# Part of the learnt activation between attention passes moves to GpSimd, and VectorE's other part comes one chunk later

## The reference

```python
h = _transformer_conv(x, src, dst, edge_attr, Wq0, bq0, ...)   # attention: out / (s + 1e-16) + x @ Ws + bs
h = jnp.where(h >= 0, h, prelu_a * h)
h = _transformer_conv(h, src, dst, edge_attr, Wq1, bq1, ...)
h = jnp.where(h >= 0, h, prelu_a * h)
h = _transformer_conv(h, src, dst, edge_attr, Wq2, bq2, ...)
```

## Time and profile before

| | us |
|---|---|
| median of three runs (lowest, highest) | 6334.99 (6330.81, 6335.18) |
| the profiled execution | 6323.52 |
| its span | 6321.9 |
| TensorE busy in it | 5535.2 (88%) |
| VectorE busy | 5521.8 (87%) |
| GpSimd busy | 4377.9 (69%) |
| ScalarE busy | 2824.9 (45%) |

### The profile page before, as it was taken

One profiled execution on the slowest core, in us unless ns is written; L12 is line 12 of the kernel. 1 busy time (PEld: TensorE's weight loads), 2 busy tenths in 40 slices (PEclk: granted clock), 3 DMA queues, 4 the chain that ended last, 5 costly groups with the idle time before them and its releaser, 6 DMA issues. The chain is left out here.

```text
span 6321.9 us, 195360 instructions
## 1 busy us (share of the span) xinstructions
PE 5535.2 (88%) x49413; PEld 4085.5 (65%) x49413; DVE 5521.8 (87%) x18582; ACT 2824.9 (45%) x12163; POOL 4377.9 (69%) x4735
## 2 busy tenths in 40 slices
PE   7997888898988887898888889888898888898887
PEld 5775666666666666666666666666666666666665
DVE  6557999989999998998989998988899898989898
ACT  3223555555555555455555555555333333333332
POOL 1223777777777775777777777775777777777775
PEclk9998999999999998999999999999899999999998
DMA  4554433333444343433333333343433343434343
GB/s 127 159 159 112 104 101 100 101 101 101 101 102 103 101 101 101 102 103 101 102 101 101 103 101 101 101 101 96 107 103 102 101 102 101 103 101 101 101 103 80
DMA packets 732932, 662.41 MB, mean 105 GB/s; under 512 B 421004, under 2 KB 558158, under 8 KB 732878
## 3 DMA queue, kind: packets, MB, share of 16 engines
q0 software_dynamic: 148544, 293.76, 19.3%
q1 hardware_dynamic: 555242, 315.06, 18.8%
q10 hardware_dynamic: 29092, 52.97, 2.8%
HBM read 639.39 MB, written 21.78 MB: 105 GB/s over the span
## 5 line engine op out<-in xcount | busy, mean ns | idle before, releaser
L1918 POOL DMA_INDIRECT Gall<-KV,sdn x4440 | 4227.0, 952 | 1376.7 <-issue 1261.8
L1215 ACT ACTIVATE vals<-vj,vals 128x32 f32<-128x32 f32 (+1 forms) x7960 | 1796.8, 313 | 19.3
L1153 PE MATMUL pG<-KVH,ohB 128*128 128x512 f32 (+1 forms) x2586 | 1185.3, 462 | 207.0 <-DVE cont L886 171.3
L1208 ACT ACTIVATE vals<-dd 128x16 f32<-128x16 f32 (+1 forms) x606 | 131.8, 218 | 2686.7 <-DVE dd L1021 2669.6
L1153 PE MATMUL pG<-KVH,ohA 128*128 128x512 f32 (+1 forms) x2613 | 1137.5, 435 | 11.5 <-DVE fm L974 0.6
L1153 PE MATMUL pG<-KVL,ohB 128*128 128x512 f32 (+1 forms) x2586 | 1080.6, 418 | 0.0
L1153 PE MATMUL pG<-KVL,ohA 128*128 128x512 f32 (+1 forms) x2613 | 1019.8, 393 | 0.0
L1146 PE MATMUL pY<-O,vals 128*66 128x42 f32 (+1 forms) x10576 | 783.3, 237 | 0.0
L1153 PEld LDWEIGHTS pG<-KVH,ohB 128*128 128x128 f32 x2586 | 534.2, 207 | 367.3 <-issue 245.0
L1146 PEld LDWEIGHTS pY<-O,vals 128*66 128x66 f32 (+1 forms) x10576 | 710.3, 144 | 46.6 <-ACT vals L1222 34.1
L1153 PEld LDWEIGHTS pG<-KVH,ohA 128*128 128x128 f32 x2613 | 504.6, 193 | 150.8 <-issue 10.9
(11 more groups left out here) (266 smaller groups left out, 8473.0 us busy)
## 6 DMA issues: line engine op xcount, KB each, us to landing
db<-D SPq DMA_DIRECT2D x606, 256.0 KB, 3.5
ea<-in_ea SPq DMA_DIRECT2D x606, 128.0 KB
Gall<-KV,sdn POOLq DMA_INDIRECT x4440
db<-D ACTq DMA_DIRECT2D x202, 256.0 KB, 3.6
qw<-QT SPq DMA_DIRECT2D x1818, 5.2 KB
dr<-in_dr SPq DMA_DIRECT2D x1212, 4.0 KB
ea<-in_ea SPq DMA_DIRECT2D x202, 64.0 KB, 3.6
sdn<-in_sdn SPq DMA_DIRECT2D x606, 12.0 KB
```

The source lines that it names most:

```text
L1153: p = e.matmul(pG[:, 0:128 * m], table[:, n, :], half[:, 4 * q:4 * q + m, :].rearrange("p t c -> p (t c)"), start=n == 0 and h == 0, stop= ...
L1208: return e.activation(vals[u][:, :, 64:64 + H], dd[:, :, 0:H], ACT.Exp, scale=scale)
L1215: i = e.activation(vals[u][:, j, C * h:C * h + C], vj[u][:, j, C * h:C * h + C], ACT.Identity, scale=vals[u][:, j, 64 + h:65 + h])
L1918: e.indirect_dma_start(G[u][:, j, :], None, kvtab, bass.IndirectOffsetOnAxis(ap=sdn[u][:, j:j + 1], axis=0)).then_inc(s_g[u], 16)
```

## The change

`neg` goes from VectorE to GpSimd, behind the two memsets of its chunk, and waits there for VectorE's `val`. `act` leaves `fold_V_ops` and becomes `act_V`, which VectorE runs for chunk n - 1 after the fold of chunk n; it waits for GpSimd's `neg` of chunk n - 1. TensorE's columns of a chunk wait for `act`, as before. GpSimd's memset `one` waits for the `neg` of the chunk before instead of its `clr`, and in the kinds other than `mid` nothing changes.

```diff
-        fold_V = ["den", "rcp", "avg", "val"] + {"mid": ["neg", "act"]}.get(kind, ["xr"])
-        end_V = fold_V[-1]
+        fold_V = ["den", "rcp", "avg", "val"] + {"mid": []}.get(kind, ["xr"])
+        end_V = "act" if kind == "mid" else fold_V[-1]
...
-                oG += [(o, c) for c in fo for o in (("one", "clr") if kind == "mid" else ("clr",))]
+                oG += [(o, c) for c in fo for o in (("one", "clr", "neg") if kind == "mid" else ("clr",))]
                 for c in fo:
                     oP += [("ftr", c)]
                     oV += [(o, c) for o in fold_V]
+            if kind == "mid":
+                oV += [("act", c) for c in co]
...
                 if kind == "mid":
                     if c:
-                        e.wait_ge(own["G"], pG_["clr", c - 1])
+                        e.wait_ge(own["G"], pG_["neg", c - 1])
                     e.memset(hT[64:128, 512 * c:512 * c + 128 * tiles_of[c]], 1.0).then_inc(own["G"], 1)
                     e.wait_ge(own["G"], pG_["one", c])
                 e.memset(acc[:, 512 * c:512 * c + 128 * tiles_of[c]], 0.0).then_inc(own["G"], 1)
+                if kind == "mid":
+                    e.wait_ge(own["V"], pV["val", c])
+                    e.tensor_scalar(SQ[:, cells(c), :], WK[:, cells(c), :], 0.0, pra[:, 0:1],
+                                    ALU.min, ALU.mult).then_inc(own["G"], 1)
...
                 if folds:
                     for c in fo:
                         fold_V_ops(e, c)
+                if kind == "mid":
+                    for c in co:
+                        act_V(e, c)
...
-            else:
-                e.tensor_scalar(skip, val, 0.0, pra[:, 0:1], ALU.min, ALU.mult).then_inc(own["V"], 1)
-                e.wait_ge(own["V"], pV["neg", c])
-                e.scalar_tensor_tensor(val, val, 0.0, skip, ALU.max, ALU.add).then_inc(own["V"], 1)
+
+        def act_V(e, c):
+            e.wait_ge(own["G"], pG_["neg", c])
+            e.scalar_tensor_tensor(WK[:, cells(c), :], WK[:, cells(c), :], 0.0, SQ[:, cells(c), :],
+                                   ALU.max, ALU.add).then_inc(own["V"], 1)
```

More of the change, by code:

```diff
@@ L713, in fold_V_ops @@
             e.tensor_tensor(val, val, skip, ALU.add).then_inc(own["V"], 1)
-            e.wait_ge(own["V"], pV["val", c])
+            if kind != "mid":
+                e.wait_ge(own["V"], pV["val", c])
             if kind == "mean":
```

## The result

The changed kernel takes 6427.65 us, the median of 4 runs (6424.55 to 6435.08), against 6334.51 us (6330.81 to 6335.18, 4 runs) for the kernel before: a ratio of 1.0148, 95% interval 1.0137 to 1.016. It is slower, as predicted, but by 93 us and not by 50, and outside the predicted range.

What follows compares the result with a forecast made beforehand. It took VectorE to pace the node phases, with most time in untouched edge passes. Per phase 1.1 + 23.1 + 2.2 less 1.4 gave 25 us, two phases 50: from 6334.99 to 6385 us, range 6356 to 6402.

Steps and rivals of the forecast that it cites:

- the edge passes unchanged: Attention passes over the edges: the profile after would show them as before, since the change does not touch them.
- The circle: Node phases: VectorE and TensorE no longer overlap, so a chunk takes 4.53 us at half clock, 3.33 at full.
- The sum of a phase: Each node phase: 1.1 + 23.1 + 2.2 = 26.4 us more, less 1.4 for full-clock spells: 25.
- Start: Beginning of a node phase: `act` of chunk 1 comes at 2476.3 instead of 2475.17, +1.1 us.
- Middle: From `act` of chunk 1 to chunk 11: 22.2 us becomes 45.3 at half clock, +23.1, or +11.1 at full.
- End: From `act` of chunk 11 to the first query product: 3.6 us before, +2.2 at half clock, nothing at full.
- spells at full clock: Node phases: short spells of TensorE at full clock give back 1 to 2 us a phase; 1.4 taken off.
- The clock: TensorE in the node phases: half clock (1.2 GHz) for most of both, at 61% busy; chance 67%.
- Full clock as a rival: TensorE at full clock from chunk 4 or sooner: 6359 us, or about 6365 rising where it rose before; chance 17%.
- GpSimd did not become the bound: Rival in the node phases: a slow `neg` of, say, 5 us makes GpSimd the bound, 38 us more, 6423; chance 4%.
- The engines in each other's way: Rival: `neg` starts ahead of `act` and holds it up, about 0.5 us 22 times, 11 us more, 6396; chance 8%.
- VectorE as the bound, not slower: Rival in the node phases: next fold independent of `act`, chunk 1.70 us, 6325 or 6328 in all; chance 4%.

Runs made afterwards that it cites:

- the last run: Kernel before plus 26 GpSimd `tensor_scalar`s in the node phases, writing a spare tile nobody reads: 6370.21 us against 6327.14, ratio 1.007.
- Undone on TensorE's side: Changed kernel with TensorE's transposes of the next sums put ahead of the columns that wait for `act`: 9805.84 us, ratio 1.0005 to the kernel before.
- made alone: Changed kernel with `neg` kept on VectorE in the fold, only `act` one chunk later: 9865.81 against 9804.37 us, ratio 1.0068; again on another chip, 1.006.

## Why the prediction missed

**The step that failed** is its first sentence on what bounds the kernel: "nearly all of it the four passes over the edges, which the change does not touch", and with it "the edge passes unchanged" at its end. The code of the passes is untouched, but their pace is GpSimd's, one gather every 1.25 us, and the gathers became slower, by 14 ns in the median and 11 in the mean. 1480 gathers a pass and three passes make a small thing large: 50.3 of the 100.6 us between the profiled executions, where the prediction had nothing. The prediction never asked what sets the pace of the passes. If it had, it would have read that an increase of 1% in one duration there weighs as much as its whole sum; that the duration would move it could not have read anywhere in the trace of before. The busy shares hide it: GpSimd was busy 69% of the span and TensorE 88%, but 1262 of the 1377 idle us before the gathers are "issue", time in which GpSimd waited for nobody.

What the runs show of it, and how firmly:
- That the passes follow the gathers where GpSimd has nothing to wait for: shown by the last run (33.3 us of passes for 34.8 more of gathers, with the old order in the phases and the clock at 0.94), though from one profile each. It is not the other way round, since on the chips with 3000 us passes the gathers were slower by the same 8 to 14 ns and the passes no longer.
- Which programs have slower gathers: of the 20 profiles, the 8 of the five programs with 26 `tensor_scalar`s on GpSimd in the node phases have medians of 955 to 958 ns, the other 12 of 944 to 947. One such instruction in a phase, 26 at the end, or 26 memsets in the phases don't do it. How many it takes between 1 and 26 was not tried.
- Why, stays open. The gathers are slower from the first, at 587 us, before any `neg` has run in that execution, so it is a matter of the program as a whole, or of what an execution leaves to the next. No run told these two apart.

**The circle was right**, in kind and in size: 4.59 us measured against 4.53. Undone on TensorE's side, it gives back 22 of 25.5 us a phase; made alone, it costs 31. Alone it costs more than in the changed kernel in the main because `neg` is then still in the fold: 4.97 us a chunk, 0.38 more.

**The sum of a phase was right**, in part by luck: 25.5 us measured, 25 predicted. Start: `act` of chunk 1 came 2489.17 - 2482.70 = 6.5 us after the phase began, against 2475.17 - 2470.00 = 5.2 before: +1.3, predicted 1.1. Middle, from there to the `act` of chunk 11 at 2534.52: 45.35 us, predicted 45.3; nine circles were 0.06 longer than predicted and the tenth, with the half chunk in its fold, took 4.07. End, from there to L580: 4.7 us, so +1.1 where the prediction had 2.2; the last table products and the query products ran at full clock again (L580 in 1.06 us, as before). In sum 1.3 + 23.1 + 1.1 = 25.5. The prediction came near it because two errors cancelled: 1.1 us too much for the end and 1.4 too much taken off for spells at full clock. The first query product began 56.5 us into the phase, 25.5 later than before, and all that follows shifted as a whole.

**The clock was right**: half clock through both phases' rounds, at 61% busy. There was no spell at full clock in them; the prediction had taken off 1.4 us a phase for such spells. Full clock as a rival did not occur. It rose only behind the rounds.

**`neg` was mis-sized but hidden.** It was taken at 0.5 us with ends of 0.3 and 1.0; it measured 1.24, outside both:

```profile
L683 POOL TENSOR_SCALAR SQ<-WK,pra x26: 817/1244/1246, 2485.1 to 4490.4; 128x256 f32<-128x256 f32 x24, 128x128 f32<-128x128 f32 x2
```

Only the last `act` of each phase waited for it, 1.2 us in both together. So GpSimd did not become the bound. In the kernel with TensorE's order mended it matters: there `act` waits for it in nearly every chunk.

**The engines in each other's way.** In the circle `act` starts before `neg`, as the prediction had it, and keeps its 0.42 us; `neg` takes 1.24 beside it, and 1.14 where no VectorE instruction runs beside it, as in the kernel with 26 at the end. The rival's 11 us were not there. Where GpSimd started first, VectorE was held up in some cases. In the kernel with 26 additions in the phases, both of VectorE's instructions are stretched in the median by 0.14 to 0.15 us against the earlier trace rows:

```profile
L725 DVE TENSOR_SCALAR SQ<-WK,pra x26: 293/494/510, 2481.1 to 4441.3; 128x256 f32<-128x256 f32 x24, 128x128 f32<-128x128 f32 x2
L727 DVE SCALAR_TENSOR_TENSOR WK<-WK,SQ x26: 373/574/581, 2481.5 to 4441.7; 128x256 f32<-128x256 f32 x24, 128x128 f32<-128x128 f32 x2
```

Two chunks of it show that the two have different partners:

```profile
2483.15 0.53 POOL L679 MEMSET acc<- 66x512 f32 x1
2483.32 0.51 DVE L725 TENSOR_SCALAR SQ<-WK,pra 128x256 f32<-128x256 f32 x1
2483.66 1.17 POOL L682 TENSOR_SCALAR spare_tile<-XR,pra 128x256 f32<-128x256 f32 x1
2483.86 0.57 DVE L727 SCALAR_TENSOR_TENSOR WK<-WK,SQ 128x256 f32<-128x256 f32 x1
...
2488.72 0.35 DVE L725 TENSOR_SCALAR SQ<-WK,pra 128x256 f32<-128x256 f32 x1
2488.78 1.30 POOL L682 TENSOR_SCALAR spare_tile<-XR,pra 128x256 f32<-128x256 f32 x1 [0.29 <-DVE WK L718]
2489.10 0.58 DVE L727 SCALAR_TENSOR_TENSOR WK<-WK,SQ 128x256 f32<-128x256 f32 x1
```

L725 is stretched where GpSimd's memset began before it, as L720 was in the earlier trace rows, and keeps its 0.35 us where only the `tensor_scalar` meets it, which begins after it. L727 begins 0.2 or 0.3 us after that `tensor_scalar` in all 24 whole chunks and takes 0.57 or 0.58 in each.

By the rule of the Trainium skill, "SBUF — State Buffer", section "Who interferes with whom", an instruction of VectorE with two inputs in SBUF and one of GpSimd that reads SBUF shut each other out for the whole of the earlier one, which for the first L727 above would be 0.97 us. The trace agrees that there is a price and disagrees on its size, 0.15 us. In the changed kernel L722, with two inputs in SBUF, begins and ends within a `neg` that began 0.69 us earlier, in its usual 0.42:

```profile
2485.11 1.15 POOL L683 TENSOR_SCALAR SQ<-WK,pra 128x256 f32<-128x256 f32 x1 [0.38 <-DVE dn L713]
...
2485.80 0.42 DVE L722 TENSOR_TENSOR WK<-WK,SQ 128x256 f32<-128x256 f32 x1
```

**VectorE as the bound, not slower**, was rightly given little: the records L561, L571, L545 follow each other in every round.

## What to carry to other kernels

Before an instruction is delayed to take it off a busy engine, follow what the other engines do in order behind its reader: here the transposes that feed the next fold stood behind it, and to save 0.39 us on VectorE a chunk became one of 4.59 us, at half clock, instead of 2.09 at the old kernel's steady pace and full clock. And before a part of the kernel is called untouched, read what sets its pace: where one engine issues thousands of like instructions with nothing to wait for, a per cent on each is a per cent of the kernel, and work added to that engine elsewhere has to be tried and read in their median duration, not reasoned away. The engine's busy share does not show that; its idle time with nobody named as releaser does. Work on GpSimd is dear: what VectorE does in 0.35 us took it 1.24.

## What the runs showed of the hardware

- A GpSimd `tensor_scalar` on 128x256 32-bit numbers takes 1.14 us alone and 1.24 where VectorE's `act` began 0.18 us before it; that is 3.3 and 3.5 times VectorE's 0.35. GpSimd's own memset of that length took 0.31.
- A VectorE instruction with two inputs in SBUF that began 0.2 to 0.3 us after such a `tensor_scalar` took 0.57 to 0.58 us instead of 0.43; one that began 0.69 us after it took its usual 0.42.
- The median gather on GpSimd takes 944 to 947 ns or 955 to 958, by the program, in all three passes alike.
- The kernel before ran in 6335 us in the first comparison, in 6327 in the last and in 9727 to 9804 on other chips. The difference is in the attention passes, where gathers wait for transfers; its two `mid` phases take 55.7 to 56.0 us wherever they were profiled.
